# Scores of a head from one 97-row product, packed by transfers, in a gated cross-attention layer with a feed-forward part

## What is computed

```python
# x (2, 2048, 512), ctx (2, 128, 512); 16 heads of 32; _layernorm on x first
xn, kvn = layer_norm(x, g_x, b_x), layer_norm(ctx, g_kv, b_kv)
q = (xn @ w_q).reshape(B, N1, 16, 32);  k, v = split(kvn @ w_kv)
attn = softmax(where(mask == 0, -1e9, q.k * 32 ** -0.5))
x = x + tanh(g_xattn) * ((attn @ v) @ w_proj + b_proj)
# then, on layernorm of the new x: weights from integers and scales
x = x + tanh(g_ffn) * (h + 0.5 * (silu(hn @ w1 + b1) @ w2 + b2))
```

## Time and profile before

| | |
|---|---|
| median of three runs | 1220.83 us (1220.67 to 1221.43) |
| span of the profiled execution | 1219.2 us |
| TensorE busy | 1164.7 us, 96% |
| VectorE busy | 675.6 us, 55% |
| ScalarE busy | 413.7 us, 34% |
| GpSimd busy | 385.3 us, 32% |
| mean granted TensorE clock | 0.992 |
| moved by transfers | 64.89 MB, 53 GB/s |

### The profile page before, as it was taken

How to read it: one execution, slowest core, us unless ns; L and a number is a source line. 1 busy time by engine, 2 the same in 40 slices (tenths; PEclk the granted TensorE clock), 3 DMA queues, 4 the chain that set the end, 5 groups by cost and what they waited for, 6 DMA issues and landing times.

```text
span 1219.2 us, 16062 instructions
## 1 busy us (share of the span) xinstructions
PE 1164.7 (96%) x5817; PEld 912.6 (75%) x5817; DVE 675.6 (55%) x953; ACT 413.7 (34%) x650; POOL 385.3 (32%) x381
## 2 busy tenths in 40 slices
PE   5588999999999997899999999999999999999998
PEld 3355777777776765688888888888888888888887
DVE  6778877877779576777445235235235235245222
ACT  3476666666665662333111111111112111111110
POOL 5554765766657555220112012012012012012000
PEclk9899999999999999999999999999999999999999
DMA  7110022121221135930200200100100200200000
GB/s 246 35 53 1 19 87 70 51 72 34 86 69 36 52 104 164 306 151 1 70 1 1 69 1 1 69 2 0 69 0 0 69 0 1 69 1 1 35 1 35
DMA packets 32377, 64.89 MB, mean 53 GB/s; under 512 B 2456, under 2 KB 2624, under 8 KB 31808
## 3 DMA queue, kind: packets, MB, share of 16 engines
q1 hardware_dynamic: 31560, 63.98, 15.9%
q10 hardware_dynamic: 760, 0.14, 0.1%
HBM read 47.34 MB, written 16.78 MB: 53 GB/s over the span
## 4 chain that ended last, share of the span: by engine, by line
PE 59%; DVE 1%; issue 0%; ACT 0%; DVEq 0%
PE ps_y L220 10%; PE ps_y L219 10%; PE ps_z L1185 10%; PE ps_z L1187 10%; PE ps_z L1186 10%; PE ps_y L218 10%; PE ps_h L1199 1%; DVE x_in L1305 0%; DVE x L1268 0%; DVE y_hi L1245 0%; DVE w_lo L176 0%; DVE w_f L170 0%; ACT w_hi L161 0%; DVE y_lo L1247 0%; DVEq L47 0%
## 5 line engine op out<-in xcount | busy, mean ns | idle before, releaser
L1245 DVE CAST y_hi<-y_f 128x512 fp32r<-128x512 f32 x128 | 63.2, 494 | 391.6 <-ACT y_f L1220 391.6
L1220 ACT ACTIVATE y_f<-ps_y,cols 128x512 f32<-128x512 f32 x128 | 87.9, 687 | 552.9 <-PE ps_y L220 552.9
L1185 PE MATMUL ps_z<-w_hi,y_hi 128*128 128x512 f32 x512 | 203.3, 397 | 3.0 <-DVE w_lo L176 3.0
L218 PE MATMUL ps_y<-xt_hi,w_hi 128*128 128x512 f32 x512 | 202.0, 395 | 2.3 <-PEq L254 2.3
L220 PE MATMUL ps_y<-xt_hi,w_lo 128*128 128x512 f32 x512 | 203.4, 397 | 0.0
L219 PE MATMUL ps_y<-xt_lo,w_hi 128*128 128x512 f32 x512 | 202.9, 396 | 0.0
L1187 PE MATMUL ps_z<-w_hi,y_lo 128*128 128x512 f32 x512 | 200.7, 392 | 0.0
L1186 PE MATMUL ps_z<-w_lo,y_hi 128*128 128x512 f32 x512 | 200.4, 391 | 0.0
L753 DVE RECIPROCAL inv_den<-ps_den 128x512 f32<-128x512 f32 x32 | 107.1, 3348 | 47.0 <-PE ps_den L483 47.0
L218 PEld LDWEIGHTS ps_y<-xt_hi,w_hi 128*128 128x128 f32 x512 | 96.2, 188 | 25.4 <-issue 2.7
L1185 PEld LDWEIGHTS ps_z<-w_hi,y_hi 128*128 128x128 f32 x512 | 96.5, 189 | 23.8 <-DVE w_lo L176 3.4
(11 more groups left out here) (172 smaller groups left out, 1863.9 us busy)
## 6 DMA issues: line engine op xcount, KB each, us to landing
x_in<-in_x SPq DMA_DIRECT2D x8, 1024.0 KB, 6.4
x_res<-in_x SPq DMA_DIRECT2D x32, 256.0 KB, 2.9
x_dram<-x_out SPq DMA_DIRECT2D x32, 256.0 KB, 3.1
q_raw<-in_L_ffn_fc_q SPq DMA_DIRECT2D x8, 1024.0 KB, 14.8
s_raw<-in_L_ffn_fc_scales SPq DMA_DIRECT2D x8, 1024.0 KB, 16.1
x_in<-x_dram SPq DMA_DIRECT2D x4, 1024.0 KB, 6.0
x<-x_dram SPq DMA_DIRECT2D x4, 1024.0 KB, 5.5
out<-x_in SPq DMA_DIRECT2D x4, 1024.0 KB, 4.2
```

The lines of the kernel that those rows point to most:

```text
L218: nc.tensor.matmul(out, s_hi, m_hi, start=(k == 0), stop=False)
L1185: nc.tensor.matmul(ps_z[t][:, :], hi, w2_hi[:, f, :], start=(f == 0), stop=False)
L1220: nc.scalar.activation(y_f[f % 2][:, :], ps_y[f % 2][:, :], ACT.Silu, bias=b1_c[:, f:f + 1]).then_inc(y_f_ready, 1)
```

## The change

- The queries of a unit are still split into q_hi and q_lo, now in two buffers each. SyncE copies them, with 12 transfers of 32 rows (64 KB) each, into `q_pack`, which holds for each head q_hi, q_lo and q_hi again below one another, 96 rows, and with 4 transfers of one row each the head's maxima as row 97. `k_pack` holds the high part of the keys twice, their low part, and -1 in row 97; it is filled once, by 12 transfers, as is k_hi by 4. The scores of a head are one product of 97 rows.
- q_f and GpSimd's q_lo go. VectorE takes q_lo straight from the bank ps_qm, after the second pair of maxima and ahead of the row statistics.
- The maxima are turned into ps_max[1] instead of ps_qm; the queries no longer wait for the rows of maxima, and the second maxima product does.
- The sums are turned in 32 x 32 blocks out of their bank (a sum stands 32 times below itself), one value of each 32 is inverted, and the result is turned back.
- In the set-up the zeroing of k_lo, the constants of the maxima, and the separate low and high parts of batch 1's keys (in steps 1 and 3) go.

```diff
+        q_pack = [sb(f"q_pack{n}", [P, HG, CHUNK], F32R) for n in range(2)]
@@ SyncE, at the end of each step
+                if real(i, k + 1, UNITS):
+                    pack_maxima(i, k + 1)
+                if real(i, k + 2, UNITS):
+                    pack_queries(i, k + 2)
+            def pack_maxima(i, k):
...
+                after(sp, max_row_ready, v + 1)
+                for j in range(HG):
+                    sp.dma_start(q_pack[k % 2][3 * HEAD:PACK, j, :].bitcast(F32),
+                                 max_row[k % 2][j:j + 1, :].bitcast(F32)).then_inc(max_packed[k % 2], 16)
+            def pack_queries(i, k):
...
+                after(sp, q_hi_ready, v + 1)
+                after(sp, q_lo_ready, v + 1)
+                after(sp, s_done, HG * (v - 1))
+                for n, part in enumerate((q_hi, q_lo, q_hi)):
+                    for j in range(HG):
+                        sp.dma_start(q_pack[k % 2][head_rows(n), j, :].bitcast(F32), part[k % 2][head_rows(j), :].bitcast(F32)
+                                     ).then_inc(q_packed[k % 2], 16)
+            def pack_keys():
+                sp.wait_ge(k_top_ready, 1)
...
+            every_step(sp, step, {-8: load_context, -7: load_weights, -3: pack_keys})
@@ SyncE, ahead of the first x_res
+                    sp.wait_ge(wq_lo_ready, 2)
+                    sp.wait_ge(wp_lo_ready, 1)
@@ TensorE
             def queries(i, k, blocks):
-                    after(pe, q_f_ready, v)
-                    after(pe, max_row_ready, v - 1)
+                    after(pe, q_lo_ready, v)
             def scores_for_max(i, k, tiles):
+                    if t == 1:
+                        after(pe, max_row_ready, v)
             def scores(i, k, j):
                 if j == 0:
-                    after(pe, q_lo_ready, v + 1)
-                    after(pe, max_row_ready, v + 1)
+                    after(pe, q_packed[k % 2], 16 * 3 * HG * (before_in_slot(i, k) + 1))
+                    after(pe, max_packed[k % 2], 16 * HG * (before_in_slot(i, k) + 1))
                 after(pe, p_hi_ready, HG * v + j - 1)
-                nc.tensor.matmul(to, k_hi[:, b, m, j, :], q_hi[k % 4][:, :], start=True, stop=False)
-                nc.tensor.matmul(to, k_hi[:, b, m, j, :], q_lo[k % 4][:, :], start=False, stop=False)
-                nc.tensor.matmul(to, k_lo[:, b, m, j, :], q_hi[k % 4][:, :], start=False, stop=False)
-                nc.tensor.matmul(to, minus_row[:, j, :], max_row[k % 2][:, :], start=False, stop=True).then_inc(s_done, 1)
+                nc.tensor.matmul(ps_s[j % 2][:, :], k_pack[0:PACK, j, m, b * KEYS:(b + 1) * KEYS], q_pack[k % 2][0:PACK, j, :],
+                                 start=True, stop=True).then_inc(s_done, 1)
@@ ScalarE
             def take_queries(i, k):
-                after(act, s_done, HG * (v - 3))
+                after(act, q_packed[k % 2], 16 * 3 * HG * before_in_slot(i, k))
...
-                nc.scalar.activation(q_f[k % 2][:, :], ps_qm[:, :], ACT.Identity, scale=SCALE).then_inc(q_f_ready, 1)
             def take_maxima(i, k):
-                after(act, s_done, HG * (v - 1))
+                after(act, max_packed[k % 2], 16 * HG * before_in_slot(i, k))
@@ VectorE
+            def queries_lo(i, k):
+                after(dve, q_hi_ready, v + 1)
+                after(dve, q_packed[k % 2], 16 * 3 * HG * before_in_slot(i, k))
+                nc.vector.scalar_tensor_tensor(out=q_lo[k % 2][:, :], in0=ps_qm[:, :], scalar=SCALE,
+                                               in1=q_hi[k % 2][:, :].bitcast(F32), op0=ALU.mult, op1=ALU.subtract
+                                               ).then_inc(q_lo_ready, 1)
             def invert_sums(i, k):
+                nc.vector.transpose(den_t[:, :, :], ps_den[:, :]).then_inc(den_turned, 1)
+                after(dve, den_turned, v + 1)
+                nc.vector.reciprocal(inv_t[:, :, :], den_t[:, :, 0:1]).then_inc(den_inv_t, 1)
+                after(dve, den_inv_t, v + 1)
                 after(dve, o_f_ready, v)
-                nc.vector.reciprocal(inv_den[:, :], ps_den[:, :]).then_inc(den_inv, 1)
+                nc.vector.transpose(inv_den[:, :], inv_t[:, :, :].to_broadcast([P, CHUNK // HEAD, HEAD])).then_inc(den_inv, 1)
             def step(i, k):
+                if real(i, k + 2, UNITS):
+                    queries_lo(i, k + 2)
@@ VectorE, set-up
+                nc.vector.tensor_copy(k_top[:, :, :], k_full[:, :, :]).then_inc(k_top_ready, 1)
```

More of the change, by code:

```diff
@@ L259, in sem @@
             return scope.enter_context(nc.semaphore(name))
-        q_f = [sb(f"q_f{n}", [P, CHUNK], F32) for n in range(2)]
-        q_hi = [sb(f"q_hi{n}", [P, CHUNK], F32R) for n in range(4)]
-        q_lo = [sb(f"q_lo{n}", [P, CHUNK], F32R) for n in range(4)]
+        q_hi = [sb(f"q_hi{n}", [P, CHUNK], F32R) for n in range(2)]
+        q_lo = [sb(f"q_lo{n}", [P, CHUNK], F32R) for n in range(2)]
+        q_pack = [sb(f"q_pack{n}", [P, HG, CHUNK], F32R) for n in range(2)]
         with ExitStack() as early:
@@ L383, in step @@
                 tile = k - 4
+                if isinstance(i, int) and PER * i + tile == 0:
+                    sp.wait_ge(wq_lo_ready, 2)
+                    sp.wait_ge(wp_lo_ready, 1)
                 if real(i, tile, UNITS):
@@ L439, in scores_for_max @@
                     after(pe, max_taken, TT * v + t - 1)
-                    nc.tensor.matmul(ps_max[t % 2][:, :], q_hi[k % 4][:, t * P:(t + 1) * P],
-                                     k_hi[:, b, m, :, :].rearrange("p j n -> p (j n)"),
+                    if t == 1:
+                        after(pe, max_row_ready, v)
+                    nc.tensor.matmul(ps_max[t % 2][:, :], q_hi[k % 2][:, t * P:(t + 1) * P],
+                                     k_hi[:, m, b, :, :].rearrange("p j n -> p (j n)"),
                                      start=True, stop=True).then_inc(max_done, 1)
@@ L446, in turn_maxima @@
                 after(pe, max_taken, TT * (v + 1))
-                after(pe, q_f_ready, v + 2 if real(i, k + 1, UNITS) else v + 1)
-                after(pe, max_row_ready, v)
                 for t in range(TT):
-                    last = nc.tensor.transpose(ps_qm[0:HG, t * P:(t + 1) * P], maxima[k % 2][:, t, :], ident[:, :])
+                    last = nc.tensor.transpose(ps_max[1][0:HG, t * P:(t + 1) * P], maxima[k % 2][:, t, :], ident[:, :])
                 last.then_inc(max_turned, 1)
@@ L620, in take_queries @@
                 after(act, q_done, v + 1)
-                after(act, s_done, HG * (v - 3))
-                nc.scalar.activation(q_hi[k % 4][:, :], ps_qm[:, :], ACT.Identity, scale=SCALE).then_inc(q_hi_ready, 1)
-                after(act, q_lo_ready, v - 1)
-                nc.scalar.activation(q_f[k % 2][:, :], ps_qm[:, :], ACT.Identity, scale=SCALE).then_inc(q_f_ready, 1)
+                after(act, q_packed[k % 2], 16 * 3 * HG * before_in_slot(i, k))
+                nc.scalar.activation(q_hi[k % 2][:, :], ps_qm[:, :], ACT.Identity, scale=SCALE).then_inc(q_hi_ready, 1)
             def probabilities(i, k, j):
@@ L652, in take_maxima @@
                 after(act, max_turned, v + 1)
-                after(act, s_done, HG * (v - 1))
-                nc.scalar.copy(max_row[k % 2][0:HG, :], ps_qm[0:HG, :]).then_inc(max_row_ready, 1)
+                after(act, max_packed[k % 2], 16 * HG * before_in_slot(i, k))
+                nc.scalar.copy(max_row[k % 2][:, :], ps_max[1][0:HG, :]).then_inc(max_row_ready, 1)
             def outputs_hi(i, k):
@@ L721, in values_second_part @@
                     nc.scalar.copy(v_parts[1][:, b, :], v_rest[:, b, :]).then_inc(v_second, 1)
-            def second_keys_hi():
-                act.wait_ge(k_hi_ready, 1)
-                for j in range(HG):
-                    at = slice(HEAD * j, HEAD * (j + 1))
-                    last = nc.scalar.copy(k_hi[at, 1, :, j, :], k_full[at, :, KEYS:2 * KEYS])
-                last.then_inc(k_hi_ready, 1)
             def last_steps(u):
@@ L918, in last_steps @@
                     g("weights")(dve, 0, (u - UNITS) // 2)
-            every_step(dve, step, {-8: context_rows, -7: masks, -4: lambda: [key_parts(), key_means()], -3: lambda: keys_lo(0),
-                                   0: value_parts, 3: lambda: keys_lo(1)})
+            every_step(dve, step, {-8: context_rows, -7: masks, -4: lambda: [key_parts(), key_means()], 0: value_parts})
         @block.gpsimd
         def _(pool):
-            def queries_lo(i, k):
-                v = PER * i + k
-                after(pool, q_f_ready, v + 1)
-                after(pool, s_done, HG * (v - 3))
-                nc.gpsimd.tensor_tensor(q_lo[k % 4][:, :], q_f[k % 2][:, :], q_hi[k % 4][:, :].bitcast(F32),
-                                        ALU.subtract).then_inc(q_lo_ready, 1)
             def bias_residual(i, k):
@@ L1050, in first_outputs @@
                 pool.wait_ge(bias_scaled, 1)
[L1051 to L1053 removed]
```

(1 more changed line is left out.)

111 lines of the change are left out of this document (56 added, 55 removed).

## The result

| | before | after |
|---|---|---|
| median of the runs | 1221.13 us (1220.67 to 1222.21) | 1248.5 us (1246.29 to 1250.92) |
| span of the profiled execution | 1219.2 us | 1244.7 us |
| first feed-forward matmul | 488.44 us | 515.40 us |
| mean granted TensorE clock | 0.992 | 0.961 |

The account below looks back on a forecast made before the run. TensorE was taken to bound the attention part before 488 us. Gains of 1.6 (five chunks), 5.7 (last four full units) and 6.0 (tail) made 13.3: 1205.9 us profiled, 1207.5 as a median; range 1186 to 1231.

Parts of the forecast that it names:

- The plain unit: Four heads of one chunk, without a load stall: period 11.21 us instead of 12.70, bound by the wait for ScalarE's exponentials.
- The inversion: On VectorE, two block turns and a reciprocal of 16 values replace the 3345 ns reciprocal: 1.5 us, bounds 1.4 to 2.8.
- the term of SyncE's queue: Twelve query issues at 0.36 us, 4.3 us, delay the load of x; TensorE idles 3.55 us once per chunk.
- rival 2: Same late load of x, slower: 0.50 us an issue and landing in 7.4 give 1227 us; chance 0.25.
- The clock's loss: TensorE's matmuls run at the 1.2 GHz level after each load stall: 1.8 us charged, range 1.2 to 2.4.
- The five chunks: From unit 8, each chunk takes 50.55 us against 50.80, 0.3 gained each, 1.6 us in all.
- Start-up to unit 8: Savings on batch 1's keys and units without projection offset late loads of some 4 and 6 us: zero net.
- the tail: Last attention units run on exponentials, p_lo and weighted values, 8.1 us instead of 10.0, about twice, plus 1.84: 6.0 gained.
- the weights' issue behind the last packings: Feed-forward weights on SyncE have tens of us before use, so it is covered; uncovered, up to 10 us.
- if the scores themselves wait for q_pack: Sign in TensorE's score products, waiting for the packed queries and maxima, that would show the prediction wrong; no size given.
- rival 4: TensorE isn't unloaded because 97 rows cost what four products did: about 1243 us; chance 0.01 of the slower 0.25.
- Rival 3: Packing transfers still drain when the load of x is issued, 1.4 us later per load: 1217 us; chance 0.12.

Follow-up runs that it names:

- the thin transfers: The changed kernel with every packing transfer cut from 512 to 64 columns, same number and order of transfers: 1244.63 us.
- e4: The kernel before, computing all it did, with sixteen unread transfers a unit added to SyncE's queue where the changed kernel packs: 1306.0 us, ratio 1.069.
- the last kernel: Load of x first and maxima in one transfer (1183.9 us), plus the first feed-forward weight load moved behind the last packing of maxima: 1175.09 us, ratio 0.963.
- e1: The changed kernel with the load of x issued ahead of the twelve packing transfers, none added or removed: 1192.08 us, ratio 0.977 to the kernel before.
- e7: The kernel with the load of x first (1192.1 us), its four one-row transfers of maxima made one of four rows: 1183.85 us, ratio 0.969.

## Why the prediction was wrong

**What held.** The plain unit was forecast at 11.21 and is 11.23; the wait that takes TensorE's place is the one for p_hi, 0.64 us at a time. The inversion was put at 1.5 (bounds 1.4 to 2.8): the turn takes 0.71 us, the reciprocal of 16 values 0.25 and the turn back 0.71, and one inversion runs from 216.59 to 218.34, 1.75 us. q_lo was 0.68, measured 0.69. The mechanism too was the forecast's: load behind twelve issues, VectorE stands, TensorE stands, clock falls. With the load first and the maxima in one transfer the change is worth 38 us, 30 of it TensorE's.

**The step that failed is the term of SyncE's queue.** I took 0.36 us an issue, bounds 0.31 and 0.50, from transfers out of the device's memory; the packing goes from on-chip to on-chip:

```profile
L442 SPq DMA_DIRECT2D q_pack<-q_hi x62: 517/590/1523, 199.5 to 295.8; - x62
```

With the gap that is 7.5/12 = 0.625 apart, beyond even my rival 2's decision point of 0.52. Twelve make 7.5, not 4.3. A second, smaller piece: I started the twelve 1.1 us before the unit's end; they started 0.5 before it (221.33 against 221.82), since the four for the maxima stood ahead until 221.14. So the load went out at +7.2 instead of +3.2 and landed at +13.2 instead of +9.5 (the landing itself, 5.9, was near the 6.3 taken); VectorE stood 7.74 instead of 4.3, TensorE 6.95 instead of 3.55. The clock's loss was sized right: from q_hi to q_hi this unit takes 20.1 us, of which 11.2 are a plain unit's and 6.95 the stall; 1.9 are left, against 1.8 charged. Rival 2 had this place and this sign, and its own price, 0.50, was too low as well.

**By the milestones.** The profiled execution was forecast at 1205.9 and took 1244.7, 38.8 more. The five chunks: forecast -1.6, measured +18.2. Start-up to unit 8: forecast 0, by two late loads of 4 and 6 us against 5.8 saved; measured +7.5; the two units with the late loads are 8.7 and 10.0 us longer than before, where 4 and 6 were charged. The last units: -4.3 for three, measured -4.7. The end: forecast -6.0 for the tail and 1.4 for the last unit, together -7.4, measured +5.9. Here a second step failed. I wrote that the weights' issue behind the last packings is covered, and looked only at who waits for the weights; the last packing of maxima stands behind the weights, and the scores waited 9.31 us for it. I had named "if the scores themselves wait for q_pack" as what would make the prediction wrong, and they did, once.

The tail was mis-sized too. With the weights behind the packing the end is 49.2 us against 51.6, 2.4 shorter and not 7.4. I had put two of the last units at 8.1 us in place of 10.0; in that kernel the weighted values of the last two units start 10.07 apart:

```profile
413.04 1.47 PE L532 MATMUL ps_o<-p_hi,v 128*32 128x512 f16 x12 [1.88 <-POOL p_lo L992]
...
423.11 1.30 PE L532 MATMUL ps_o<-p_hi,v 128*32 128x512 f16 x12 [1.92 <-POOL p_lo L992]
```

The interval before it is 8.95. Behind the wait at 413.04 the granted clock is 0.51 (window 413 to 416), the 1.2 GHz level, where the kernel before had 1.00 at this place (458 to 461). From the first of these products to the first scores it takes 3.10 us (to 416.14), and took 1.63 before (458.22 to 459.85). So about 1.5 of the 2 us missing here are the clock, which I had charged only to the load's stalls. TensorE had stood 1.88 us ahead of it, and 1.74 in the kernel before; why the clock fell in one and not in the other, these runs don't show.

**Sums.** Three small slips in the prediction change nothing: 5 x 0.3 is 1.5, not 1.6; the tail's twice 1.9 and 1.84 make 5.6, not 6.0; rival 4's sum gives 1245, not 1243.

**Rival 3**, the transfers still draining, falls with the thin transfers: 64 KB land in 2.0 us (median; the longest of the 384 took 3.5), 8 KB in 1.8, and the time moves by 4 us only. The Trainium skill's figure (DMA: Bandwidth & Descriptors, Bandwidth) made twelve take an estimated 5.7 us; they are issued over 7.5, so by that figure too the issue, not the transfer, is slow.

**Open.** Why an issue sometimes takes 1.4 to 1.9 us (maximum 1523 ns above); how much of e4's surplus is VectorE's order rather than the low clock; and the half of the last kernel's 8.8 us that its two profiled executions don't show.

## What to carry to other kernels

Price a DMA's issue from a row with the same source and the same neighbour in the queue, multiply by the count, and write down what stands behind the last of them; sixteen at 0.6 us take 10 of a unit's 11 us on an engine that looked idle. When a queue gets many issues, put the one load that a busy engine waits for ahead of them (here 56 us for one change of order) and look at both directions at every hand-over: who waits for what I issue late, and whose bytes do I put ahead of the small transfer that is needed now. A part that removes a bound is only seen once the new waits are cured: the same change was 1.022 of the time before, then 0.977, 0.969 and 0.963.

## What the runs showed of the hardware

- An issue on SyncE took 0.59 us for an on-chip source behind an on-chip one, 0.50 to 0.53 behind one from memory or behind a pause; from memory it took 0.33 to 0.41 behind memory, 0.34 behind a pause. Behind another on-chip one, 128 rows, 32 rows, one row (in the packing), and 512 or 64 columns all took 0.59. One transfer of four rows took 0.64.
- A 1 MB load landed after 5.6 to 6.4 us with twelve transfers of 64 KB issued behind it (e1) and after 6.0 to 8.4 with the same twelve in e7, while the kernel before, with none, had 5.2 to 7.4: no price for sharing shows. But 2 KB issued right behind the weights landed 7.8 to 9.5 us after issue, against 2.1 elsewhere.
- On VectorE a turn of 128 x 512 in 32 x 32 blocks took 0.71 us, out of PSUM and from a broadcast source alike; the reciprocal took 0.25 us for 16 values a row and 3.35 for 512.
